# Reordering the end of cross attention in a two-attention and experts kernel

## Chip, cores, metric

The kernel runs on one core of one Trainium2 chip. The metric is the device time of one execution in microseconds. All data is float32; products that need more than one pass are split into a high part and a low part by hand ("hi" and "lo"), and `product` (L41 to L45) issues three matmuls for one: hi by hi, hi by lo, lo by hi.

## The reference, cut to what matters

The reference is one transformer layer over x (8 batches, 128 tokens, 512 features): cross attention to a context of 2048 tokens, then a differential self attention, then a mixture of eight experts, each on a layer norm of x and added to x. The change lies in the end of the first and the start of the second.

```python
q = (LN(x) @ wq.T + bq)       # 8 x 128 x 512, 16 heads of 32
k = ctx @ wk.T + bk           # 8 x 2048 x 512
v = ctx @ wv.T + bv
attn = softmax(q @ k.T / sqrt(32))
x = x + (attn @ v) @ wo.T + bo
lam = exp(sum(lq1 * lk1)) - exp(sum(lq2 * lk2)) + 0.8     # per head
x = x + differential_attention(LN(x), lam, rms_scale, ...)
x = x + experts(LN(x), ...)
```

## The kernel before

Cross attention is one stage (`cross_attention`). Its work is cut into 32 slots: slot m is batch m // 4 and head group m % 4 (four heads). A slot has four chunks of 512 keys, so there are 128 chunks; chunk n belongs to slot n // 4. Each chunk passes through these steps:

- scores on PE (`column_scores`, L852): 32 matmuls into the one PSUM tile `psS`;
- a running maximum on VectorE (L1083, L1086): four instructions;
- the move of the scores to SBUF on ScalarE (L1029), into one of seven buffers; then `psS` is free;
- subtraction of the maximum on VectorE (L1050), exponential on ScalarE (L1012);
- value product on PE (`outputs`, L866), accumulated over the four chunks of a slot in `psO`. The denominators come from sums on GpSimd (L761, L766) and a matmul per slot (L889) up to slot 27, and for the last four slots (`TAIL`) from matmuls of their own (L880), two by two with the value products.

The maximum of a slot is turned on PE (M, L897), reduced on VectorE (L1059), spread on ScalarE (L1007), turned back (B, L897) and copied to `mb` (L980). A slot is finished by a reciprocal (L1071) and a product (L1075) on VectorE, and a copy with the value bias on ScalarE (L1019), whose result is stored to a scratch tensor.

Nothing plans this at run time. Each engine's block runs over the same counter `beat`, and within a beat issues its steps in the order in which they are written. The functions `score_step`, `move_step`, `exp_step`, `value_steps`, `normal_slot` and the like say which chunk or slot has a step in this beat. Each engine works through its own queue in order and waits on semaphores. While projections of new keys and values run, they fill PE. From beat `LATE` (slot 32 of the projections, which isn't there) on, only ten score steps are left (chunks 118 to 127), and the room is used for the output projection: the output weight is turned in four blocks (W, `turn_weight`, L904) at the beats in `W_BEAT`, evicted by ScalarE (L984, L985) and split by GpSimd (L745); the attention output of batches 0 to 6 is loaded back from the scratch tensor, split by ScalarE (L999, beats in `O_BEAT`) and GpSimd (L751), and projected by PE (Y, `project_tile`, beats in `Y_BEAT`) into a work bank, which ScalarE evicts (L989). From `LATE` on two banks are used in turn, as the third holds the denominators. GpSimd adds bo to x (L741) and at the end adds the projected tiles to it (`add_tile`, L514).

The next stage, `output_projection`, begins when all engines have ended the first. It projects the tile of batch 7, makes the statistics and the layer norm in two halves (`Norm`, L166 to L212), turns the result (L1096) and splits it (L1215, L1226). Lambda (`lam_*`) is computed in it too. Then come the projections of the self attention (L1336 and on).

## Time and profile before

| | us |
|---|---|
| median of 3 runs | 1677.9 |
| lowest and highest | 1677.11, 1684.54 |
| the profiled execution | 1679.28 |
| its span | 1677.5 |
| PE busy in the span | 1608.8 (96%) |
| VectorE busy | 1166.9 (70%) |
| ScalarE busy | 954.1 (57%) |
| GpSimd busy | 932.3 (56%) |

PE is nearly full over the span as a whole, but not everywhere: from 1047 to 1176 us, where cross attention ends and the next stage runs, it is busy 90 of 129 us. This is the part that the change touches. In the profile PE is TensorE, DVE is VectorE, ACT is ScalarE and POOL is GpSimd; the granted clock of TensorE is a share of its full speed.

### The profile page before, as it was taken

The numbers are of one execution on the slowest core, as the hardware profiler recorded it, in microseconds if no ns is written. First come the engines' busy times: TensorE is split into PE (matmuls) and PEld (weight loads), VectorE is DVE, ScalarE is ACT, GpSimd is POOL, SyncE is SP. The second block draws the span as 40 slices with busy tenths as digits, with TensorE's granted clock in tenths as the row PEclk, the third lists the DMA queues.
The fourth block names the chain that finished last, engine by engine and source line by source line (L and its number), as shares of the span: only waits on it lengthen the run. The fifth ranks groups of instructions, "written<-read, shape, count | busy, mean of one in ns | idle before, by whom it ended". The sixth has DMA issues, their size and how long they took to land. (4 is left out here: it accounts for less than half of the span.)

```text
span 1677.5 us, 36990 instructions
## 1 busy us (share of the span) xinstructions
PE 1608.8 (96%) x15556; PEld 1302.3 (78%) x15556; DVE 1166.9 (70%) x1506; ACT 954.1 (57%) x1445; POOL 932.3 (56%) x498
## 2 busy tenths in 40 slices
PE   7999999999999999999999999677998899999999
PEld 6788888888888888888888888566886677777787
DVE  6137888888888888888888887756434677653322
ACT  4347677777677776777776776753102777630000
POOL 1227788788888878888887885322000344522220
PEclk9999999999999999999999999778999999899999
DMA  8422222222222222222222211203432111211001
GB/s 179 96 40 39 35 42 36 36 38 40 39 38 38 36 36 41 40 36 38 38 39 37 42 23 61 74 3 108 163 88 88 58 45 52 66 51 50 29 22 51
DMA packets 333876, 88.61 MB, mean 53 GB/s; under 512 B 284656, under 2 KB 317168, under 8 KB 333712
## 3 DMA queue, kind: packets, MB, share of 16 engines
q1 hardware_dynamic: 333712, 86.26, 23.0%
q8 instruction: 123, 2.02, 0.5%
q14 instruction: 41, 0.34, 0.1%
HBM read 71.60 MB, written 14.61 MB: 51 GB/s over the span
## 5 line engine op out<-in xcount | busy, mean ns | idle before, releaser
L766 POOL TENSOR_TENSOR b_acc<-b_acc,b_s 128x1024 f32<-128x1024 f32 x168 | 562.8, 3350 | 12.4 <-ACT b_s L1012 5.5
L1050 DVE TENSOR_TENSOR b_s<-b_s,b_mb 128x2048 f32<-128x2048 f32 x128 | 395.9, 3094 | 32.5 <-ACT b_mb L980 32.5
L1086 DVE TENSOR_TENSOR b_mx<-b_psS,b_mx 128x512 f32<-128x512 f32 x480 | 330.8, 689 | 103.0 <-PE b_psS L852 90.0
L1012 ACT ACTIVATE b_s<-b_s 128x2048 f32<-128x2048 f32 x128 | 244.3, 1909 | 13.8 <-DVE b_s L1050 10.6
L1029 ACT ACTIVATE b_s<-b_psS 128x2048 f32<-128x2048 f32 x128 | 241.1, 1884 | 15.9 <-DVE b_mx L1086 15.9
L43 PE MATMUL b_work<-wvT,cT 128*128 128x512 f32 x496 | 203.2, 410 | 0.0
L43 PE MATMUL b_work<-cT,wkT 128*128 128x512 f32 x496 | 200.2, 404 | 1.7 <-POOL b_ones L732 1.7
L44 PE MATMUL b_work<-cT,wkT 128*128 128x512 f32 x496 | 194.3, 392 | 0.0
L44 PE MATMUL b_work<-wvT,cT 128*128 128x512 f32 x496 | 194.2, 392 | 0.0
L45 PE MATMUL b_work<-wvT,cT 128*128 128x512 f32 x496 | 193.4, 390 | 0.0
L45 PE MATMUL b_work<-cT,wkT 128*128 128x512 f32 x496 | 193.2, 389 | 0.0
L735 POOL TENSOR_TENSOR cT<-cin,cT 128x512 fp32r<-128x512 f32 x120 | 155.8, 1299 | 54.7 <-ACT cT L1004 54.7
L952 ACT ACTIVATE b_kT<-b_work,b_bk 128x512 f32<-128x512 f32 x124 | 85.4, 689 | 141.1 <-PE b_work L45 141.1
L852 PE MATMUL b_psS<-b_q,b_kT 32*128 32x128 f32 x4096 | 152.9, 286 | 12.2 <-ACT b_s L1029 12.1
L852 PEld LDWEIGHTS b_psS<-b_q,b_kT 32*128 32x128 f32 x4096 | 128.4, 189 | 38.1 <-issue 38.1
L761 POOL TENSOR_TENSOR b_acc<-b_s 128x1024 f32<-128x1024 f32 x28 | 68.7, 2452 | 129.5 <-PE b_psO L889 127.6
L866 PE MATMUL b_psO<-b_s,v_sb 128*32 128x128 f32 x4096 | 128.1, 276 | 0.6 <-issue 0.6
L866 PEld LDWEIGHTS b_psO<-b_s,v_sb 128*32 128x32 f32 x4096 | 109.4, 111 | 22.7 <-issue 22.6
L43 PEld LDWEIGHTS b_work<-cT,wkT 128*128 128x128 f32 x496 | 93.0, 187 | 27.5 <-POOL b_ones L732 2.1
L1040 DVE STREAM_TRANSPOSE cin<-cin 128x512 f32<-128x512 f32 x120 | 83.8, 699 | 41.7 <-DMA b_bv<-in_L_xattn_bv 19.3
L43 PEld LDWEIGHTS b_work<-wvT,cT 128*128 128x128 f32 x496 | 93.0, 188 | 24.5
L1846 ACT ACTIVATE e_sm<-e_psS,e_low 128x128 f32<-128x128 f32 x256 | 89.9, 382 | 34.5 <-DVE e_low L1921 34.5
(315 smaller groups left out, 2815.8 us busy)
## 6 DMA issues: line engine op xcount, KB each, us to landing
cin<-in_ctx SPq DMA_DIRECT2D x496, 64.0 KB, 2.4
experts_sb<-in_L_ffn_expert_w SPq DMA_DIRECT2D x8, 1024.0 KB, 5.4
q_scratch<-d_st SPq DMA_DIRECT2D x16, 256.0 KB, 2.3
k_scratch<-d_st SPq DMA_DIRECT2D x16, 256.0 KB, 2.3
e_q<-q_scratch SPq DMA_DIRECT2D x16, 256.0 KB, 2.7
k_sb<-k_scratch SPq DMA_DIRECT2D x16, 256.0 KB, 2.9
b_kT<-in_x SPq DMA_DIRECT2D x4, 512.0 KB, 7.5
q_scratch<-a_q SPq DMA_DIRECT2D x8, 256.0 KB, 2.3
```

The source lines that it names most:

```text
L43: nc.tensor.matmul(out, lhs[0], rhs[0], start=first, stop=False)
L44: nc.tensor.matmul(out, lhs[0], rhs[1], start=False, stop=False)
L45: return nc.tensor.matmul(out, lhs[1], rhs[0], start=False, stop=last)
L735: nc.gpsimd.tensor_tensor(cT[1][:, p % 2, k, :], cin[:, 1, k % 2, :], f32(cT[0][:, p % 2, k, :]), ALU.subtract).then_inc(split_done, 1)
L766: nc.gpsimd.tensor_tensor(acc[:, :, :], acc[:, :, :], s[:, buf, 2 * i:2 * i + 2, :], ALU.add).then_inc(sum_done, 1)
L852: last = nc.tensor.matmul(psS[:, j, t * P:(t + 1) * P], kT[h, at + t * P:at + (t + 1) * P], q[h, m % 3, :], start=True, stop=True)
L866: last = nc.tensor.matmul(psO[j * HD:(j + 1) * HD, 0:P], v[:, at + j * HD:at + (j + 1) * HD], s[:, n % BUFS, i, j * P:(j + 1) * P], start= ...
L1012: nc.scalar.activation(part, part, ACT.Exp, scale=SCALE).then_inc(exp_done, 1)
L1029: nc.scalar.activation(s[:, n % BUFS, :, :].rearrange("p t (j q) -> p t j q", j=HG), psS[:, :, :].rearrange("p j (t q) -> p t j q", t=CHUN ...
L1050: nc.vector.tensor_tensor(s[:, n % BUFS, :, :], s[:, n % BUFS, :, :], mb[:, :].rearrange("p (o n) -> p o n", o=1).broadcast_to([P, CHUNK, ...
L1086: nc.vector.tensor_tensor(mx[:, :, :], part, mx[:, :, :], ALU.max).then_inc(mx_done, 1)
L1846: last = nc.scalar.activation(sm[:, hf, i, j % 2, u, :], psS[:, j, u, :], ACT.Exp, bias=low[:, hf, j, u:u + 1], scale=-1.0, accum_out=sums ...
```

## The change

- On PE, from beat `LATE` on the scores of a beat are issued ahead of its value products and denominators.
- On ScalarE the evictions of W and Y and the high halves of O go behind the move of the scores in a beat, where they stood at its head.
- The beats of W, O and Y are others. W comes four beats earlier.
- Tiles 0 to 5 and not 0 to 6 are projected in cross attention; tiles 6 and 7 in the next stage. Tiles 0 to 3 are evicted by ScalarE and added by GpSimd as before (0 and 1 in the late beats), tiles 4 and 5 are added straight out of PSUM by VectorE.
- The last maximum is reduced ahead of a subtraction, not behind it.
- The last chunk is subtracted and exponentiated in two halves, and its denominators are issued ahead of its value products.
- The lambda loads, product, sum and exponential, and a first use of the square root, are in cross attention; statistics of tiles 0 to 3 too, where it was 0 and 1. `Lambda` holds the tensors.

```diff
-        W_BEAT = {0: LATE + 5, 1: LATE + 5, 2: LATE + 7, 3: LATE + 7}
-        O_BEAT = {0: LATE + 8, 1: LATE + 9, 2: LATE + 12, 3: LATE + 13, 4: LATE + 15, 5: LATE + 17, 6: LATE + 20}
-        Y_BEAT = {0: LATE + 12, 1: LATE + 16, 2: LATE + 19, 3: LATE + 20, 4: LATE + 21, 5: LATE + 23, 6: LATE + 25}
-        TILES = B - 1
+        W_BEAT = {0: LATE + 1, 1: LATE + 1, 2: LATE + 3, 3: LATE + 3}
+        O_BEAT = {0: LATE + 5, 1: LATE + 7, 2: LATE + 9, 3: LATE + 11, 4: LATE + 13, 5: LATE + 17, 6: LATE + 21}
+        Y_BEAT = {0: LATE + 8, 1: LATE + 12, 2: LATE + 16, 3: LATE + 18, 4: LATE + 20, 5: LATE + 23}
+
+        TILES, ADDED = B - 2, 4
+
+        def parts(n):
+
+            if n < SLOTS * CHUNK - 1:
+                return [slice(0, CHUNK)]
+            return [slice(0, CHUNK // 2), slice(CHUNK // 2, CHUNK)]
...
@@ SP, at beat LATE + 2, behind the loads of o_sb
+                    for i, name in enumerate(("lq1", "lq2", "lk1", "lk2")):
+                        sp.dma_start(consts.lam_in_sb[:, i, :], w_next[name]).then_inc(consts.lam_in, 16)
...
@@ GpSimd
-                    for t in {LATE: (0, 1), LATE + 2: (2, 3), LATE + 4: (4, 5), LATE + 6: (6, 7)}.get(beat, ()):
-                        bias(t)
-                    for k in {LATE + 8: (0, 1), LATE + 10: (2, 3)}.get(beat, ()):
-                        weight_lo(k)
-                    for t in {LATE + 12: (0, 1), LATE + 14: (2, 3), LATE + 16: (4,), LATE + 18: (5,)}.get(beat, ()):
-                        output_lo(t)
-                if beat == LATE + 20:
+                    for work_of, n in {
+                            0: ((bias, 0), (bias, 1), (bias, 2)), 2: ((weight_lo, 0), (weight_lo, 1), (bias, 3)),
+                            4: ((weight_lo, 2), (weight_lo, 3)), 6: ((output_lo, 0), (bias, 4), (bias, 5)),
+                            8: ((bias, 6), (bias, 7), (output_lo, 1)), 10: ((output_lo, 2),),
+                            12: ((output_lo, 3), (add, 0)), 14: ((output_lo, 4),),
+                            16: ((add, 1),), 18: ((output_lo, 5),)}[beat - LATE]:
+                        work_of(n)
+                if beat == LATE + 22:
                     output_lo(6)
 
-            pool.wait_ge(sub_done, SLOTS * CHUNK)
-            for t in range(4):
-                add_tile(nc, pool, shared, t)
+            pool.wait_ge(sub_done, SLOTS * CHUNK + 1)
+            for t in range(2, ADDED):
+                add(t)
...
@@ PE
+            def last_outputs(n):
+
+                for i in range(0, CHUNK, 2):
+                    pe.wait_ge(exp_done, n + 1 + i // 2)
+                    for t in range(i, i + 2):
+                        last = tile_denominators(n, t)
+                    if i + 2 == CHUNK:
+                        last.then_inc(last_sums, 1)
+                    for t in range(i, i + 2):
+                        last = tile_outputs(n, t)
+                last.then_inc(pv_done, 1)
...
             for beat in range(FIRST, LAST):
+                if beat >= LATE and (n := score_step(beat)) is not None:
+
+                    column_scores(n)
                 for n in value_steps(beat):
-                    outputs(n)
+                    if n < SLOTS * CHUNK - 1:
+                        outputs(n)
+                    else:
+                        last_outputs(n)
                 if (m := sum_slot(beat)) is not None and m < TAIL:
                     denominators(m)
-                if (n := score_step(beat)) is not None:
+                if beat < LATE and (n := score_step(beat)) is not None:
                     column_scores(n)
...
@@ ScalarE: evictions of W, of Y below ADDED, and the O halves now behind the move in a beat; at the end
+            act.wait_ge(consts.lam_step, 2)
+            nc.scalar.activation(consts.lam_e[:, :], consts.lam_s[:, :], ACT.Exp).then_inc(consts.lam_exp, 1)
+            nc.scalar.activation(norm.root[:, :], ident[:, 0:B], ACT.Sqrt)
...
@@ VectorE
+            def add_tile(t):
+                dve.wait_ge(work_full, RING["Y", t, 0] + 1)
+                dve.wait_ge(shared.bo_done, t + 1)
+                nc.vector.tensor_tensor(x1[:, t, :], work[BANK["Y", t, 0]][:, :], x1[:, t, :], ALU.add).then_inc(y_added, 1)
...
             for beat in range(FIRST, LAST):
+                if (m := spread_slot(beat)) == SLOTS - 1:
+                    reduce_maximum(m)
                 if (n := exp_step(beat)) is not None:
...
-                if (m := spread_slot(beat)) is not None:
+                if (m := spread_slot(beat)) is not None and m < SLOTS - 1:
+                    reduce_maximum(m)
                 if (m := normal_slot(beat)) is not None:
                     if m == SLOTS - 1:
+                        for t in range(ADDED, TILES):
+                            add_tile(t)
+                        dve.wait_ge(consts.lam_in, 16 * 4)
+                        nc.vector.tensor_tensor(consts.lam_p[:, :, :], consts.lam_in_sb[:, 0:2, :],
+                                                consts.lam_in_sb[:, 2:4, :], ALU.mult).then_inc(consts.lam_step, 1)
                         for t in range(2):
...
+                    elif m < SLOTS - 1:
+                        dve.wait_ge(pv_done, (m + 1) * CHUNK)
                     else:
-                        dve.wait_ge(pv_done, (m + 1) * CHUNK)
+                        dve.wait_ge(last_sums, 1)
...
@@ the next stage, PE
+            for g in range(G):
+                last = product(nc, bank[0][:, :], [a[:, g, :] for a in shared.o_half[THERE % 4 - 2]],
+                               [a[:, g, :] for a in woT], g == 0, g == G - 1)
+            last.then_inc(full, 1)
             pe.wait_ge(o_lo, 2)
...
@@ the next stage, VectorE
-            for t in range(2, THERE):
-                dve.wait_ge(shared.y_done, t + 1)
-                norm.tile_stats(x1, t)
-            dve.wait_ge(lam_in, 16 * 6)
...
-            for t in range(THERE, LAST):
-                dve.wait_ge(shared.y_done, t + 1)
+            for t in range(B // 2, THERE):
                 norm.tile_stats(x1, t)
-            dve.wait_ge(shared.bo_done, B)
-            dve.wait_ge(full, 1)
-            nc.vector.tensor_tensor(x1[:, LAST, :], bank[0][:, :], x1[:, LAST, :], ALU.add).then_inc(lo_done, 1)
-            dve.wait_ge(lo_done, 1)
-            norm.tile_stats(x1, LAST)
+            for t in range(THERE, B):
+                dve.wait_ge(full, t - THERE + 1)
+                nc.vector.tensor_tensor(x1[:, t, :], bank[t - THERE][:, :], x1[:, t, :], ALU.add).then_inc(lo_done, 1)
+                dve.wait_ge(lo_done, t - THERE + 1)
+                norm.tile_stats(x1, t)
```

## Rows read from the trace of the kernel before

**Rows 1.** Busy time of each engine by stage; columns: busy us (instructions), clock, DMA share, GB/s.

```profile
1047.57:1116.37 68.80, 49.41 (x989) 42.30 (x985) 49.26 (x53) 45.21 (x43) 21.39 (x17) 0.78 0.18 47
1116.37:1129.67 13.30, 8.40 (x64) 6.74 (x61) 5.57 (x7) 6.96 (x7) 2.55 (x2) 0.87 0.00 0
1129.67:1151.84 22.17, 20.39 (x425) 17.64 (x424) 12.78 (x10) 10.28 (x10) 5.02 (x4) 1.00 0.06 15
1151.84:1169.33 17.49, 7.88 (x28) 6.41 (x28) 13.56 (x43) 4.79 (x11) 4.62 (x7) 0.79 0.68 240
1169.33:1176.08 6.75, 4.19 (x19) 3.81 (x19) 5.86 (x14) 2.39 (x4) 0.00 (x0) 0.50 0.01 2
```

**Rows 2.** Waits by total, 1047 to 1178 us: total us, times, longest.

```profile
ACT b_s L1029 <- DVE b_mx L1086: 15.9, 7, 3.0
...
PE b_psS L852 <- ACT b_s L1029: 12.1, 6, 5.0
```

**Rows 3.** Timeline of PE: start us, us, engine, line, operation, count, idle before.

```profile
1053.82 1.17 PE L852 MATMUL b_psS<-b_q,b_kT 32*128 32x128 f32 x32 [1.03 <-ACT b_s L1029]
...
1059.98 2.09 PE L852 MATMUL b_psS<-b_q,b_kT 32*128 32x128 f32 x32 [0.82 <-ACT b_s L1029]
...
1070.25 1.09 PE L904 MATMUL b_work<-ident,wo_sb 128*128 128x128 f32 x8
...
1076.75 1.93 PE L866 MATMUL b_psO<-b_s,v_sb 128*32 128x128 f32 x32 [0.27 <-issue]
...
1091.94 0.77 PE L43 MATMUL b_work<-woT,b_o_half 128*128 128x512 f32 x1 [0.49 <-POOL b_o_half L751]
...
1097.20 1.08 PE L866 MATMUL b_psO<-b_s,v_sb 128*32 128x128 f32 x32
...
1140.05 0.39 PE L43 MATMUL b_work<-woT,o_half 128*128 128x512 f32 x1
...
1142.86 1.08 PE L866 MATMUL b_psO<-b_s,v_sb 128*32 128x128 f32 x32
```

**Rows 4.** Timeline of VectorE, cross attention's end.

```profile
1036.41 3.21 DVE L1050 TENSOR_TENSOR b_s<-b_s,b_mb 128x2048 f32<-128x2048 f32 x1 [1.12 <-ACT b_mb L980]
...
1047.70 0.96 DVE L1071 RECIPROCAL b_rD<-b_psO 128x128 f32<-128x128 f32 x1 [1.21 <-PE b_psO L889]
...
1055.05 2.87 DVE L1086 TENSOR_TENSOR b_mx<-b_psS,b_mx 128x512 f32<-128x512 f32 x4 [1.09 <-PE b_psS L852]
1057.84 2.28 DVE L1050 TENSOR_TENSOR b_s<-b_s,b_mb 128x2048 f32<-128x2048 f32 x1
1060.04 0.68 DVE L1059 TENSOR_REDUCE b_top<-b_work 128x4 f32<-128x512 f32 x1
```

**Rows 5.** Timeline of GpSimd, its last additions of the steady part.

```profile
1035.06 6.79 POOL L766 TENSOR_TENSOR b_acc<-b_acc,b_s 128x1024 f32<-128x1024 f32 x2 [5.30 <-ACT b_s L1012]
```

**Rows 6.** Timeline of ScalarE in the ring.

```profile
1057.95 1.88 ACT L1029 ACTIVATE b_s<-b_psS 128x2048 f32<-128x2048 f32 x1 [2.05 <-DVE b_mx L1086]
...
1061.29 1.90 ACT L1012 ACTIVATE b_s<-b_s 128x2048 f32<-128x2048 f32 x1
1063.15 0.60 ACT L980 ACTIVATE b_mb<-b_work 128x512 f32<-128x512 f32 x1
...
1067.28 0.60 ACT L985 ACTIVATE woT<-b_work 128x512 fp32r<-128x512 f32 x1
```

**Rows 7.** Timelines of VectorE and ScalarE in the next stage.

```profile
1153.81 1.35 DVE L1232 TENSOR_TENSOR c_oT<-b_o,c_oT 128x128 fp32r<-128x128 f32 x1
1155.08 1.27 DVE L166 BATCH_NORM_STATS2 c_norm_stats<-x 128x6 f32<-128x512 f32 x2
1157.14 0.21 DVE L1238 TENSOR_TENSOR c_lam_p<-c_lam_in 16x64 f32<-16x64 f32 x1 [0.79 <-DMA e_rs<-in_L_attn_rms_scale]
...
1164.01 0.67 DVE L1252 TENSOR_TENSOR x<-c_ps,x 128x512 f32<-128x512 f32 x1
...
1157.85 1.28 ACT L208 ACT_TABLE_LOAD   x1
```

More of the change, by code:

```diff
@@ L749, in output_lo @@
                 pool.wait_ge(shared.o_hi, t + 1)
+                if t == 1:
+                    pool.wait_ge(shared.bo_done, B)
                 hi, lo = o_half[t % 4]
@@ L811, in wait_evicted @@
                         pe.wait_ge(shared.wo_hi, m + 1)
+                    elif kind == "Y" and m < ADDED:
+                        pe.wait_ge(shared.y_moved, m + 1)
                     elif kind == "Y":
-                        pe.wait_ge(shared.y_moved, m + 1)
+                        pe.wait_ge(y_added, m - ADDED + 1)
                     else:
@@ L863, in outputs @@
                 for i in range(CHUNK):
[L864 to L869 removed]
+                    last = tile_outputs(n, i)
@@ new lines, in tile_outputs @@
+            def tile_outputs(n, i):
+                m, c = divmod(n, CHUNK)
+                b, g = divmod(m, G)
+                at = value_places(b, c * CHUNK + i)[g]
+                for j in range(HG):
+                    last = nc.tensor.matmul(psO[j * HD:(j + 1) * HD, 0:P],
+                                            v[:, at + j * HD:at + (j + 1) * HD],
+                                            s[:, n % BUFS, i, j * P:(j + 1) * P],
+                                            start=c == 0 and i == 0, stop=c == CHUNK - 1 and i == CHUNK - 1)
+                return last
@@ L883, in chunk_denominators, with tile_denominators @@
+            def tile_denominators(n, i):
+                c = n % CHUNK
+                for j in range(HG):
+                    last = nc.tensor.matmul(work[BANKS - 1][j * HD:(j + 1) * HD, 0:P], ones[:, :],
+                                            s[:, n % BUFS, i, j * P:(j + 1) * P],
+                                            start=c == 0 and i == 0, stop=c == CHUNK - 1 and i == CHUNK - 1)
                 return last
```

161 lines of the change are left out of this document (80 added, 81 removed).

## Prediction

> I write S118 to S127 for the last ten score steps (32 score matmuls each, L852), O for one chunk's value product with its denominators, Y for the projection of one batch tile, W for the turning of one block of the output weight, M29 and B29 for the turns of the maxima of slot 29. A step's "move" is ScalarE's copy of the scores out of PSUM (L1029).
>
> **What bounds the kernel now.** I read first the busy time by stage. The change touches only the end of cross attention and the stage behind it, and five stretches hold it [rows 1]: S118 to S127 (68.80 us, granted clock 0.78), S127 to the subtraction of chunk 124 (13.30), from there to the last copy of the attention output (22.17), the next stage to its first low half (17.49), and its rest (6.75). No engine is full in the first: PE 49 us of 69, VectorE 49, ScalarE 45. So it is bound by a chain, and the waits name it: ScalarE waits for the maxima, PE for the move [rows 2]. There is one PSUM tile for scores, so the chain is a ring: scores, maxima, move, next scores. The shortest turn stands in the timeline: S119 starts at 1053.82, the maxima at 1055.05 and last 2.87, the move runs from 1057.95 for 1.88, S120 starts at 1059.98 [rows 3, 4, 6]. That is 1.23 + 2.90 + 2.03 = 6.16 us; nine turns are 55.4 of the 68.8. The other 13.4 us are turns in which the next scores stood behind something else on PE, or the move behind something on ScalarE. The dearest is Y0 with two O in front of S125: Y0 alone is 5.26 us, from 1091.94 to 1097.20, at the low clock [rows 3].
>
> The clock matters here. Scores take 1.17 us (1053.82) or 2.09 us (1059.98, after PE had waited), twelve Y matmuls 2.81 us (1140.05 to 1142.86) or 5.26; the first half of an O takes 1.08 or 1.93 us [rows 3]. These are the 2.4 and the 1.2 GHz level.
>
> **The ring after the change.** I follow it turn by turn at full clock.
> - *Start.* S118 is issued ahead of the denominators of slot 27 and begins earlier by their 0.6 us, at 1046.99. But VectorE has the reciprocal of slot 27 in front of the maxima of 118, and that now waits for denominators behind the scores. Before, it started at 1047.70 and lasted 0.96 [rows 4]; now it starts near 1048.8, when both are done, and with the 0.3 us product behind it the maxima start at 1050.05, where they had started at 1048.90. The turn lasts 8.0 instead of 6.16: 1.8 lost.
> - *S120.* The turns W2 and W3 now stand ahead of S120, and W3 needs the PSUM bank of M29, which is free only when VectorE has subtracted chunk 115 (2.28) and reduced the maximum (0.68) [rows 4]. Eight matmuls of this kind took 1.09 [rows 3], so W3 costs 0.55. From the end of the maxima this is 2.28 + 0.68 + 0.55 = 3.5 against the move's 2.03: 1.4 lost. Queued behind PE's new wait is S120, and all engines wait for S120.
> - *The same place, a shared resource.* VectorE's subtraction takes 2.28 us alone but 3.21 at 1036.41, where GpSimd ran its additions [rows 4, 5]. The low halves of the weight now run on GpSimd just behind S119, beside the subtraction of 115. The rows bound it by 0 and 0.93; the additions cover nearly the whole subtraction, so I take the upper end, 1.0 rounded. Elsewhere the subtraction has about 1 us of room in a turn, and I cost it at nothing. (The Trainium skill, "GPSIMD: programming the Q7 cores", section Limitations, says GpSimd shares an SBUF port with VectorE. It speaks against moving additions to run beside VectorE work; the two rows agree with it.)
> - *S121.* ScalarE has exp of 115 (1.90 [rows 6]), four evictions of W2 and W3 (0.60 each, less some overlap) and the copy of mb (0.60) ahead of move 120: together 4.4 from the spread copy's end, against scores and maxima of 4.1. 0.3 lost.
> - *S122 to S127.* The O behind S121, S123 and S125 (two of them are four halves at 1.08, the first matmuls of one over the last of another: 3.5 us at full clock [rows 3]) end before the move does: scores 1.1 + 3.5 = 4.6 of 6.16. A Y behind scores ends at 1.1 + 2.8 = 3.9. O and Y halves and their evictions now lie behind the move on ScalarE. So what stood in front of S121, S123, S125 and S127 before is covered by the maxima and the move. The second O of each pair is needed seven chunks later only. Reciprocals at 122 and 126 cost 0.1 each: 0.2. GpSimd's queue has the low half for Y0 behind the weight's and S121, done near 1071 where Y0 wants it at 1076: nothing.
>
> Sum: 55.4 + 1.8 + 1.4 + 1.0 + 0.3 + 0.2 = 60.1.
>
> *The clock in the ring.* Before, three of the ten scores took the long time, S120 [rows 3] and two others like it. After, PE does the same work in fewer microseconds, with waits of 1.5 to 3 us in nearly each turn. A low S costs 0.92. I take four of nine: 3.5. The bounds are 0 and the slow rival below (8.3 and pushes). So the ring takes 63.6 and S127 starts at 1046.99 + 63.6 = 1110.6, against 1116.37: **5.8 gained**.
>
> **From S127 to the subtraction of chunk 124.** Before, M31 was issued right behind the maxima. Now two O and Y3 are ahead of it: 1.15 + 3.5 + 2.8 + 0.5 = 7.95 us after S127, where the maxima are there at 4.1. So 3.3 us are lost at M31. In return Y2 (about 4.3 of the stretch) and the evictions are gone from the front, and the maximum is reduced ahead of the subtraction. On: 0.7 reduction, 2.25 subtraction of 123, 1.95 exp (it stands ahead of mb on ScalarE), 0.55 mb: 13.4. Before 13.30 [rows 1]. **Nothing gained**; 2.3 lost if Y3 runs at the low clock.
>
> **To the last output copy.** Before 22.17. PE has two Y fewer in it ahead of the O, ScalarE no Y evictions that hold up exp. VectorE sets the end: subtractions 124 and 125 (4.5), reciprocal and product (1.25), subtraction 126 and the two halves of 127 (2.28 + 2.35, the split costs about 0.1) are 10.4. The two adds of tiles 4 and 5 (0.67 each, as the add at 1164.01), four statistics (1.27 for two [rows 7]), and two small steps make 4.2: VectorE reaches the last reciprocal at 14.6. PE is done at 13.45 (last exp half at 11.9, then three quarters of a chunk), so the early denominators hide nothing: the reciprocal would wait for VectorE's own queue. 0.96 + 0.3 + 0.4 behind: 16.3. **5.9 gained.** What is late next is VectorE, by 1.2 us.
>
> **A new piece before the stage's end.** ScalarE now does the lambda exponential, a table load and a root behind its last copy, and all engines meet at the end of the stage: 0.2 + 1.28 [rows 7] + 0.2. **1.7 lost.** Bounds 1.5 and 1.7 by the rows. (The Trainium skill, "ScalarE: Activation LUTs", section What ACT_TABLE_LOAD costs, puts a drain of 1.38 us beside the load, in all about 2.66. By it the loss would be 3.1 and the sum 1.4 us worse. The load at 1157.85 starts right behind an exponential and shows no such time.)
>
> **The next stage.** VectorE is its chain. Out of it go: two statistics 1.27, the lambda product with its wait for a transfer (0.79 + 0.5), the 1.28 of the table load, and 0.9 of the low halves, which ran beside GpSimd's additions (128 columns took 1.35) [rows 7]. In come: one more add (0.67 + 0.1), and a wait for tile 7, as PE has 24 matmuls where it had 12. They start 0.4 us into the stage at the low clock: the first twelve end at 5.6, the others at 8.4 to 9.5, where VectorE wants them at 8.2: 0.2 to 1.3; and a memset moved into the chain, 0.15. 4.7 - 0.8 - 0.15 = 3.8, less that wait, is 3.6 to 2.5; it hangs on when PE's clock comes up, and I take the middle: **3.1 gained**. The lambda loads, four issues on SP's queue, go behind the loads of the attention output and ahead of the store of slot 28, for which that queue would have waited anyway: nothing. The weight loads for the stage behind it start as before at its beginning, and nothing in rows says they'd be late. The last stretch of 6.75 stays.
>
> **The sum.** 5.8 + 0 + 5.9 - 1.7 + 3.1 = 13.1 us. The profiled execution took 1679.28 with a span of 1677.5, the median of the runs is 1677.9, 1.4 below it. 1679.3 - 13.1 = 1666.2, less 1.4: **1665 us** in terms of the median. Within 0.5% means within 8.4 us, about what a measurement of this kernel can tell from no change.
>
> **Rivals.**
> - *Clock free.* PE's work lies in shorter gaps, so that every S runs at full clock. For it: nearly every turn now has matmuls in it, and S119, with products in front of it, was fast. Against it: gaps of 1.5 to 3 us stay in each turn, and S120 was slow [rows 3]. 3.5 better: 1661.5. Chance 0.17.
> - *Clock and neighbours dearer.* About a third of the PE work of the rival below is slow, or a product pair at the low clock pushes the next S (scores 2.0 + two O 6.6 = 8.6 against a turn of 7.1: 1.5 each, five of them), and GpSimd slows more subtractions. 5 to 10 worse: 1670 to 1675. Chance 0.18.
> - *Slower than before: PE at the low clock all through.* Scores before products leave PE waiting in every turn, so it never comes up. Then nine S cost 8.3 instead of 3.5, pushes 6.0 in the ring, and behind S127 PE itself becomes the bound: scores 2.05, four pairs of O at 6.6, Y3 to Y5 at 5.26, M31, B31 and the wait between them 3.4, are 47.6 us to the last product against my 26.9 (13.4 + 13.45), of which VectorE's tail hides 1.2: 19.5 more. 4.8 + 6.0 + 19.5 = 30.3: 1695. The kernel is slower once about 13 of these 30 come. Against it: the granted clock was 0.78 in the ring with its long waits and 1.00 in the stretch with the fewest [rows 1], and at the low clock a pair of O fills its turn and leaves no gap. Chance 0.05.
> - *Forecast*, 1661 to 1669: 0.60.
>
> **Chances.** Faster by over 0.5% (below 1669.5): 0.60 + 0.17 = 0.77. Within: 0.18. Slower: 0.05. The range 1659 to 1674 takes in the first two cases with 2 us for what I haven't seen, and most of the third.
>
> **What would show it.** S118 to S127 in 60 to 66 us, turns without a low clock at 6.2, and S119 and S120 late by 1.8 and 2.4. M31 about 8 us after S127. The reciprocal of slot 31 not waiting for PE. A table load before the stage's end and 1.7 us between the last output copy and the next stage. The next stage at 14.4 up to the first low half. The prediction is wrong if PE's waits before S don't end by the move, if the clock is well under 0.8 in the ring, or if the steady loop ahead of it, untouched here, has another length.

## The result and the profile after

| | before | changed |
|---|---|---|
| median of 7 runs, us | 1683.73 | 1670.15 |
| lowest and highest | 1677.11, 1685.1 | 1666.02, 1672.92 |
| profiled execution | 1679.28 | 1670.15 |
| its span | 1677.5 | 1668.4 |

The ratio is 0.9931, with a 95% interval of 0.9908 to 0.9954: 0.69% faster, or 11.6 us of 1678 to 1684. Run again beside the experiments below, the changed kernel came to 0.9952 (0.9934 to 0.9970). Both kernels have two levels some 5 us apart, which experiment 10 looks into. One execution of the kernel before, taken beside experiments 1 and 2, was a slow one of 2024.4 us at a granted clock of 0.743 and is in no ratio.

The busy time by stage, as in [rows 1], cut at the same events (S118, S127, subtraction of 124, end of the last output copy, first low half, first matmul of the self projections). Columns: busy us (instructions) of PE, PEld, DVE, ACT, POOL, then clock, DMA share, GB/s:

```profile
1047.56:1111.78 64.22, 45.66 (x885) 38.86 (x885) 51.96 (x53) 44.90 (x42) 26.08 (x19) 0.87 0.18 50
1111.78:1126.97 15.19, 13.65 (x216) 11.57 (x220) 5.80 (x7) 8.27 (x9) 1.30 (x1) 0.89 0.01 2
1126.97:1144.04 17.07, 13.77 (x384) 11.93 (x372) 16.43 (x17) 8.76 (x9) 5.48 (x3) 1.00 0.06 17
1144.04:1158.98 14.94, 9.08 (x40) 7.38 (x40) 11.21 (x39) 4.79 (x12) 0.60 (x4) 0.89 0.68 238
1158.98:1165.52 6.54, 3.76 (x18) 3.55 (x19) 5.81 (x14) 2.39 (x4) 0.00 (x0) 0.74 0.27 101
```

Against [rows 1]: 68.80 became 64.22, 13.30 became 15.19, 22.17 became 17.07, 17.49 became 14.94, 6.75 became 6.54. From S118 to the self projections 128.51 us became 117.96: 10.55 less. S118 comes at the same time in both (1047.57 and 1047.56), although it no longer waits for 0.58 us of denominators: the steady part took 0.57 longer in this execution (in the second profile of the changed kernel, experiment 10, S118 starts at 1046.94). The span is 9.1 shorter, so 1.46 us of the 10.55 were lost behind the changed stages.

The ring on PE, with the start and length of the scores and what they waited for ([rows 3] has the like of before):

```profile
1047.56 1.17 PE L867 MATMUL b_psS<-b_q,b_kT 32*128 32x128 f32 x32
1048.66 0.65 PE L922 MATMUL b_psO<-b_acc,b_ones 128*32 128x128 f32 x16
...
1055.49 2.09 PE L867 MATMUL b_psS<-b_q,b_kT 32*128 32x128 f32 x32 [5.16 <-ACT b_s L1050]
...
1064.16 0.65 PE L937 MATMUL b_work<-ident,wo_sb 128*128 128x128 f32 x4 [0.35 <-DVE b_top L1086]
1064.75 1.17 PE L867 MATMUL b_psS<-b_q,b_kT 32*128 32x128 f32 x32
...
1070.92 2.09 PE L867 MATMUL b_psS<-b_q,b_kT 32*128 32x128 f32 x32 [2.67 <-ACT b_s L1050]
...
1085.08 2.09 PE L867 MATMUL b_psS<-b_q,b_kT 32*128 32x128 f32 x32 [2.94 <-ACT b_s L1050]
1087.09 1.94 PE L904 MATMUL b_psO<-b_s,v_sb 128*32 128x128 f32 x32
1088.80 1.93 PE L913 MATMUL b_work<-b_s,b_ones 128*32 128x128 f32 x32
...
1092.71 0.66 PE L930 MATMUL b_work<-ident,b_mx 128*128 128x128 f32 x4
1093.29 1.17 PE L867 MATMUL b_psS<-b_q,b_kT 32*128 32x128 f32 x32
...
1111.78 2.09 PE L867 MATMUL b_psS<-b_q,b_kT 32*128 32x128 f32 x32 [2.02 <-ACT b_s L1050]
```

The scores now wait for the move (ACT b_s L1050) in most turns, as they should. The nine turns are 7.93, 9.26, 6.17, 7.08, 7.08, 8.21, 6.17, 6.16, 6.16 us. The first two are the two places that were forecast: the denominators behind S118, and W3, which waits for the reduced maximum, ahead of S120. Four of the ten scores take 2.09 us, three of them in the nine turns (S119, S121, S123) and the fourth, S127, behind them. The turn of 8.21 is the pair of products at the low clock that holds up S124. It also holds the move of chunk 123 up, which needs the buffer of seven chunks before and so waits for one of these products:

```profile
1090.86 1.88 ACT L1050 ACTIVATE b_s<-b_psS 128x2048 f32<-128x2048 f32 x1 [3.13 <-PE b_work L913]
```

VectorE in the ring and behind it, with GpSimd where the two meet:

```profile
1060.43 2.93 DVE L1112 TENSOR_TENSOR b_s<-b_s,b_mb 128x2048 f32<-128x2048 f32 x1
...
1074.38 2.53 POOL L750 TENSOR_TENSOR x<-x,b_bo 128x512 f32<-128x512 f32 x2
1075.85 3.20 DVE L1112 TENSOR_TENSOR b_s<-b_s,b_mb 128x2048 f32<-128x2048 f32 x1
...
1080.16 2.86 DVE L1159 TENSOR_TENSOR b_mx<-b_psS,b_mx 128x512 f32<-128x512 f32 x4
...
1121.55 0.69 DVE L1086 TENSOR_REDUCE b_top<-b_work 128x4 f32<-128x512 f32 x1 [4.75 <-PE b_work L930]
...
1126.97 5.59 DVE L1112 TENSOR_TENSOR b_s<-b_s,b_mb 128x2048 f32<-128x2048 f32 x2 [2.54 <-ACT b_mb L1019]
1127.47 2.95 POOL L763 TENSOR_TENSOR o_half<-o_sb,o_half 128x512 fp32r<-128x512 f32 x1 [12.20 <-ACT o_half L1072]
```

VectorE waits 4.75 us for the turned maximum, which PE has behind two O and Y3. The subtractions 124 and 125 take 5.59 us where before two took 4.49, 2.28 being the time of one alone [rows 4]:

```profile
1129.67 4.49 DVE L1050 TENSOR_TENSOR b_s<-b_s,b_mb 128x2048 f32<-128x2048 f32 x2 [6.39 <-ACT b_mb L980]
```

The subtraction of 115 took 2.93 instead of 2.28. Both lie beside work of GpSimd. At the end the first subtraction keeps its pace (the second begins 2.2 us behind it, at 1129.18), GpSimd's instruction beside it takes 2.95 us where others of its kind take 1.28, and the second subtraction, begun before GpSimd ended at 1130.42, takes 3.38.

There is a third such place, in the turn S122 to S123, which took 7.08 us although S122 ran at full clock. The subtraction beside GpSimd's two additions took 3.20 us, the reciprocal and the product of slot 28 stand behind it, and so the maxima of 122 start at 1080.16, where S122, begun at 1078.00, would have allowed 1079.23 (1.23 behind, as in [rows 3, 4]). These 0.92 us are what the subtraction was too long. The second profile has the same (3.19 us, a turn of 7.07).

ScalarE at the end of the stage, with the piece that the change adds:

```profile
1143.64 0.40 ACT L1040 ACTIVATE b_o<-b_oq,b_bv 128x128 f32<-128x128 f32 x1 [3.84 <-DVE b_oq L1148]
1143.95 0.19 ACT L1076 ACTIVATE c_lam_e<-c_lam_s 16x2 f32<-16x2 f32 x1
1144.15 1.28 ACT L1077 ACT_TABLE_LOAD   x1
1145.45 0.21 ACT L1077 ACTIVATE c_norm_root<-ident 128x8 f32<-128x8 f32 x1
1146.13 0.53 ACT L1293 ACTIVATE c_oT<-o_sb 128x384 fp32r<-128x384 f32 x1 [0.47 <-ACTq L512]
```

From the end of the last output copy (1144.04) to the next stage's first instruction are 2.09 us; before, the copy ended at 1151.84 and the next stage's first instruction of ScalarE came at 1152.42, 0.58 later. So the piece costs 1.5.

### The profile page after: what moved, and what is told of

Read it like the earlier page. It is cut to its first block and busy times, and to the rows that moved or that the text cites. A ratio compares the mean times of both kernels' runs of the same rounds, so it can differ in the third digit from the quotient of the medians.

```text
span 1668.4 us, 36971 instructions
## 1 busy us (share of the span) xinstructions
PE 1603.7 (96%) x15541; PEld 1298.4 (78%) x15556; DVE 1171.9 (70%) x1510; ACT 954.5 (57%) x1444; POOL 932.4 (56%) x495
## 5 line engine op out<-in xcount | busy, mean ns | idle before, releaser
L1112 DVE TENSOR_TENSOR b_s<-b_s,b_mb 128x2048 f32<-128x2048 f32 x129 | 400.3, 3105 | 28.9 <-ACT b_mb L1019 28.9
L1050 ACT ACTIVATE b_s<-b_psS 128x2048 f32<-128x2048 f32 x128 | 241.3, 1885 | 16.5 <-DVE b_mx L1159 11.8
```

The costliest lines, as they stand in the source:

```text
L1050: nc.scalar.activation(s[:, n % BUFS, :, :].rearrange("p t (j q) -> p t j q", j=HG), psS[:, :, :].rearrange("p j (t q) -> p t j q", t=CHUN ...
L1112: nc.vector.tensor_tensor(s[:, n % BUFS, tiles, :], s[:, n % BUFS, tiles, :], mb[:, :].rearrange("p (o n) -> p o n", o=1) .broadcast_to([P ...
```

## Experiments

All stretches are cut as above: "ring" is S118 to S127, "middle" S127 to the subtraction of 124, "end" from there to the end of the last output copy, "next" to the first low half. In the changed kernel they are 64.2, 15.2, 17.1 and 14.9 us; "the piece" is all of it, from S118 to the self projections. Experiments 3 to 9 are one execution each. A time of a whole execution can't settle a microsecond here, so the stretches of one profile are the measure.

**1. PE's old order alone (e1).** The scores of a late beat go behind the products again, all else stays as changed:

```diff
-                if beat >= LATE and (n := score_step(beat)) is not None:
+                if beat >= LAST and (n := score_step(beat)) is not None:
                     column_scores(n)
...
-                if beat < LATE and (n := score_step(beat)) is not None:
+                if (n := score_step(beat)) is not None:
                     column_scores(n)
```

> The changed kernel with PE's old order (value products and denominators ahead of the scores of a beat), all else as changed. Changed kernel: S118 to S127 64.2 us, S127 to the subtraction of 124 15.2, from there to the last output copy 17.1. Theory (the order on PE is worth time because Y and two O together don't fit under the maxima and the move): S121 0.9, S123 1.3, S125 2.3, S127 1.3 us later, so the ring 68 to 70; M31 comes after Y3 alone, so the next stretch is about 12; in all 1 to 3 us slower than the changed kernel. Rival (the order costs clock, the gain is from ScalarE's order and the new beats alone): ring at 64 or shorter, with more scores at 1.17 us. Second rival (the whole gain is PE's order): back to 1678 or more.

Ratio to the kernel before 0.9945 (0.9917 to 0.9972). Its busy time by stage, ring and middle:

```profile
1048.22:1121.30 73.08, 54.01 (x1001) 45.71 (x997) 52.08 (x53) 47.36 (x44) 26.07 (x19) 0.79 0.17 44
1121.30:1131.64 10.34, 7.92 (x68) 6.14 (x64) 5.66 (x6) 5.38 (x6) 1.31 (x1) 1.00 0.01 2
```

The ring is 8.9 us longer (clock 0.79 and not higher: the rival that the order costs clock falls; so does the second, back to 1678, with a median of 1672.2), the middle 4.9 shorter, and S118 to the self projections takes 121.64, 3.7 more than in the changed kernel. The direction and the mechanism were as expected, both stretches by more than I had put, and the sum just above 1 to 3.

**2. ScalarE's old order alone (e2).** The block that evicts W and Y and makes the O halves stands at the head of a beat again:

```diff
+                for k in late_units(W_BEAT, beat - 1):
...
+                for t in [t for t in late_units(Y_BEAT, beat - 1) if t < ADDED]:
...
+                for t in late_units(O_BEAT, beat):
...
                 if (x0 := transposed(beat)) is not None:
...
                                          ACT.Copy).then_inc(s_moved, 1)
-                for k in late_units(W_BEAT, beat - 1):
...
```

> The changed kernel with ScalarE's old order (evictions of W and Y and the O halves at the head of a beat, ahead of exp and move). Theory: a move then waits for a Y that ends late: move 124 by 1.8 us (Y1), move 126 by 1.0 (Y2), small ones elsewhere; ring 66.5 to 68, the stretches behind it within 1 us. Rival (PE's order alone makes the gain, ScalarE has room): ring 64 to 65.

Ratio 0.9948 (0.9933 to 0.9964). Ring 68.76, middle 15.36; S118 to the self projections 122.62, 4.7 more. Its timeline of ScalarE shows a move (L1070 here) behind an eviction that waits for a Y:

```profile
1097.64 0.60 ACT L1028 ACTIVATE o_sb<-b_work 128x512 f32<-128x512 f32 x1 [1.29 <-PE b_work L45]
...
1098.65 1.87 ACT L1070 ACTIVATE b_s<-b_psS 128x2048 f32<-128x2048 f32 x1
```

The rival (ScalarE has room) falls; the ring is 0.8 above the upper end that I gave.

**3. Both old orders (e12).** The edits of 1 and 2 together: what is left of the change are mainly the new beats, the two tiles in the next stage, the halves and lambda.

> PE's and ScalarE's orders both as before the change, the rest (beats, tiles, halves) as changed. With PE's order alone put back the ring was 73.1 us, with ScalarE's alone 68.8, in the kernel before 68.8. Theory (a Y in front of the scores on PE also holds the move up on ScalarE, so the two orders remove the same delays in part): 73 to 76. Rival (they add): 77 to 79. Rival (each hurts only with the other one new): 69.

Its busy time by stage, ring, middle and end:

```profile
1048.08:1118.86 70.78, 50.40 (x1000) 43.14 (x997) 52.90 (x53) 45.85 (x44) 23.96 (x19) 0.81 0.17 46
1118.86:1129.20 10.34, 7.90 (x64) 6.17 (x61) 5.66 (x7) 6.54 (x7) 1.31 (x1) 0.91 0.01 2
1129.20:1146.07 16.87, 15.52 (x401) 13.52 (x399) 16.37 (x17) 8.75 (x9) 5.48 (x3) 0.95 0.07 18
```

None of the three guesses holds: the ring is 70.8, below 73 and above 69. Over the whole piece it takes 119.45 us, against 117.96 and 116.77 in two profiles of the changed kernel and 128.51 before. So the two orders that the list of the change puts first are by this one execution together worth 1.5 to 2.7 us (the two profiles of the changed kernel are themselves 1.2 apart), and the rest of it 9.1. Each order alone, with the other new, costs more (3.7 and 4.7) than both (1.5). The rows show why ScalarE's old order costs little once PE's is old too:

```profile
1115.34 0.60 ACT L1028 ACTIVATE o_sb<-b_work 128x512 f32<-128x512 f32 x1 [3.90 <-PE b_work L45]
...
1116.35 1.87 ACT L1070 ACTIVATE b_s<-b_psS 128x2048 f32<-128x2048 f32 x1
...
1118.86 1.17 PE L867 MATMUL b_psS<-b_q,b_kT 32*128 32x128 f32 x32
```

The move stands behind an eviction that waits for a Y, and still ends at 1118.22, while PE has products ahead of the next scores until 1118.86; at the two other Y of the ring the move ends 0.6 us ahead of them as well. Only the turn S119 to S120 is longer for another reason than the clock (8.85 against 8.00 in experiment 1). That the ring is even 2.3 shorter than in experiment 1 lies in the clock of PE's products: the two O behind S120, for one, take 3.7 us here and 5.3 there. And what the orders take out of the ring (70.8 to 64.2) comes back in the middle (10.3 to 15.2) for the most part; there PE has the products and tiles that it no longer does in the ring. Against the kernel before, this kernel has a ring 2.0 us longer, a middle 3.0 shorter, an end 5.3 shorter and a next stage, with its rest, 2.8 shorter.

**4. The start of the ring (e3).** The denominators of slot 27 go ahead of S118 again:

```diff
-                if beat >= LATE and (n := score_step(beat)) is not None:
+                if beat > LATE and (n := score_step(beat)) is not None:
...
-                if beat < LATE and (n := score_step(beat)) is not None:
+                if beat <= LATE and (n := score_step(beat)) is not None:
```

> Scores ahead of products only behind the first late beat: the denominators of slot 27 go ahead of S118 again. Changed kernel: S118 at 1047.56, S119 7.9 us later. Theory (the reciprocal of slot 27 in front of the maxima makes the first turn long): S118 0.6 later, first turn 6.2 to 6.9, S119 1.1 us earlier against the end of the last value projection; the rest of the ring unchanged, so S127 0.8 to 1.7 earlier. Rival (the first turn is long from the low clock of S119 alone): first turn 7.1 or more.

The first turn is 6.24 and not 7.93, as expected by the theory, at a S118 that waits 0.58 for the denominators: 1.1 net. S119 took 1.58 us, between the two levels, and the ring 61.55. The ring is 2.7 us shorter than in the first profile of the changed kernel and 1.4 shorter than in the second, where 0.8 to 1.7 were expected. The first turn accounts for 1.7; the turn behind it was 9.55 long, and the rest comes from the turns of S122 and S123 (6.36 and 6.99 instead of 7.08 and 8.21).

**5. The weight behind S120 (e5).**

```diff
-        W_BEAT = {0: LATE + 1, 1: LATE + 1, 2: LATE + 3, 3: LATE + 3}
+        W_BEAT = {0: LATE + 1, 1: LATE + 1, 2: LATE + 5, 3: LATE + 5}
```

> W2 and W3 at beat LATE + 5, behind S120. Changed kernel: S119 to S120 9.3 us. Theory (S120 waits for W3, which waits for the bank of M29, behind a subtraction that GpSimd slows): that turn 7.1 with S119 at the low clock; ring 62 to 63 instead of 64.2. Rival (ScalarE's four evictions then fall into a later turn and delay it as much): ring 64 and a longer turn S121 to S122. If S120 drops to the low clock, 0.9 of it is given back.

The turn S119 to S120 is 7.54 instead of 9.26, and no later turn grew: 6.16, 6.85 and then five of 6.16, with no slow score behind S119.

```profile
1047.59:1106.86 59.27, 42.67 (x886) 36.27 (x885) 51.26 (x53) 44.78 (x42) 32.05 (x19) 0.91 0.20 54
```

The row is the ring's busy time. It is 4.95 shorter than in the first profile of the changed kernel (3.7 than in the second), and shorter than the 62 to 63 of the theory. 1.7 are the wait for W3. Of the rest 2.05 are the turn of S123, at full clock here (0.9 against the second profile), and 0.9 the turn of S122, in which VectorE is not late this time, as the subtraction ahead of its reciprocal took 2.69 us and not 3.20. The rival (evictions delay a later turn) falls.

**6. The last maximum ahead of Y3 (e4).**

```diff
-        Y_BEAT = {0: LATE + 8, 1: LATE + 12, 2: LATE + 16, 3: LATE + 18, 4: LATE + 20, 5: LATE + 23}
+        Y_BEAT = {0: LATE + 8, 1: LATE + 12, 2: LATE + 16, 3: LATE + 19, 4: LATE + 20, 5: LATE + 23}
```

> Y3 one beat later, so that M31 stands ahead of it on PE. Theory (the turn of the last maximum behind Y3 is on the path): M31 3.0 to 3.5 us earlier behind S127, the stretch from S127 to the subtraction of 124 11.7 to 12.5 instead of 15.2, the next one 17 to 18. Rival (PE's work is the bound from S127 on, so order doesn't matter): the first shrinks and the second grows by the same.

M31 comes 6.40 us behind S127 instead of 9.13, the middle is 13.01 instead of 15.19, the end 17.57 instead of 17.07. A gain of 2.2, of which 0.5 goes: between theory and rival, nearer to the theory (against the second profile 2.3 and 0.7). It fell short because the products ahead of M31 ran mostly at the low clock in this execution: from 1111.53 to 1116.82, 5.3 us where 3.6 are enough.

**7. The root left in the next stage (e6).** The last line of ScalarE's cross attention goes:

```diff
-            nc.scalar.activation(norm.root[:, :], ident[:, 0:B], ACT.Sqrt)
```

> The first root and its table load leave the end of cross attention; the load then falls ahead of the root in the next stage. Theory: 1.5 us less between the last output copy and ScalarE's next instruction (0.6 instead of 2.1), 1.3 more in VectorE's chain of the next stage: last output copy to first low half 14.9 becomes 14.7, a draw. Rival (the next stage waits for PE's tile 7, not for VectorE, so the load is hidden there): 13.4 to 13.8. Rival by the load's drain: 1.4 us more saved than that.

"Next" is 13.44 us, not 14.94: the rival's number, though not by its reason. The table load stands in the next stage, but costs next to nothing there. The timeline of ScalarE:

```profile
1142.75 0.53 ACT L1292 ACTIVATE c_oT<-o_sb 128x384 fp32r<-128x384 f32 x1 [0.29 <-PEq L512]
...
1143.49 1.28 ACT L208 ACT_TABLE_LOAD   x1
1144.79 0.20 ACT L208 ACTIVATE c_norm_root<-c_norm_veps 128x4 f32<-128x4 f32 x1
```

and on VectorE

```profile
1145.03 0.18 DVE L187 RECIPROCAL c_norm_rstd<-c_norm_root 128x4 f32<-128x4 f32 x1 [0.46 <-ACT c_norm_root L208]
```

It starts as soon as ScalarE is free and runs while VectorE makes the low halves and the aggregates; VectorE waits 0.46 us for the root where it waits 0.27 with the table there. Before the change the load was exposed:

```profile
1159.39 0.18 DVE L187 RECIPROCAL c_norm_rstd<-c_norm_root 128x4 f32<-128x4 f32 x1 [1.21 <-ACT c_norm_root L208]
```

ScalarE had lambda's exponential in front of it, which had waited 4.49 us for VectorE. Moving that one ahead was enough; the early root costs 1.5 and saves 0.2. The load is 1.28 us in each of these places, and in each the next instruction of ScalarE starts 0.02 us behind it.

**8. GpSimd beside VectorE (e8).** The low half of tile 6 goes behind GpSimd's last adds:

```diff
-                if beat == LATE + 22:
-                    output_lo(6)
...
                 add(t)
+            output_lo(6)
```

> GpSimd makes the low half of tile 6 behind its last adds and not beside the subtraction of 124. Theory (the two engines slow each other): subtractions 124 and 125 together 4.5 us instead of 5.6, the stretch to the last output copy 16.0 instead of 17.1. Rival (PE is as late as VectorE at the end, and gaps in its own issue set it): 17 unchanged.

The subtractions 124 and 125 take 4.49 us again and the end 15.73 instead of 17.07 (16.83 in the changed kernel's second profile): the theory's numbers. In eight other profiles with the old place of this low half the end is 16.83 or 16.84 (experiments 1, 2, 4, 5, 7 and 10, and both of 9), so the 1.1 us are the 1.1 of the two subtractions. This execution also had S127 and all that is behind it at full clock: M31 at 7.60 and the middle 13.66. "Next" was 15.61: VectorE waited 0.58 us for PE's tile 7, as twelve of the stage's matmuls ran at the low clock where it was eight in the first profile.

**9. The clock (e7, e10).** Matmuls of the identity, written to columns of the output bank that nobody reads, fill PE's waits ahead of S119, S123 and S127. First 30, 16 and 10, then 16, 9 and 5:

```diff
             for beat in range(FIRST, LAST):
+                if (fill := {LATE + 2: (16, 28), LATE + 10: (9, 29), LATE + 18: (5, 30)}.get(beat)) is not None:
+                    pe.wait_ge(od_free, fill[1])
+                    for _ in range(fill[0]):
+                        nc.tensor.matmul(psO[:, 2 * P:3 * P], ident[:, :], ident[:, :], start=True, stop=True)
                 if beat >= LATE and (n := score_step(beat)) is not None:
```

> Extra matmuls of the identity into unused columns of the output bank (30 ahead of S119, 16 ahead of S123, 10 ahead of S127), read by nobody, to fill PE's waits. Theory (the clock falls because PE waits): S119, S123 and S127 take 1.17 and not 2.09 us; ring 64.2 less 2.8 is 61.4, the stretch behind it 0.7 shorter as the products run at full clock too. Rival (the clock doesn't matter on the path, or falls for another reason): ring 64 or more, scores still 2.09.

The thirty took 6.96 us where I had reckoned 4.2 (0.14 each, from the turns), and held S119 up by 2.1; the ring was 66.23. The number says nothing on the clock's price, though S119, S123 and S127 took 1.17, as expected. S120 and S121 took 2.09 here: PE waited 2.05 us for the reduced maximum ahead of W3, and W3 already ran at the low clock.

> As the run with filling matmuls, with about half of them (16, 9 and 5), as one took 0.23 and not 0.14 us and they held S119 up by 2.0 us. Theory: S119, S123 and S127 at 1.17 us without being held up; S119 at 7.9 us behind S118; ring 61 to 62, the stretch from S127 to the subtraction of 124 13.7 and not 15.2. Rival: ring 64 or more.

The timeline of PE with the smaller number:

```profile
1050.80 3.84 PE L953 MATMUL b_psO<-ident 128*128 128x128 f32 x32 [0.38 <-DVE b_oq L1152]
1055.57 1.17 PE L867 MATMUL b_psS<-b_q,b_kT 32*128 32x128 f32 x32 [0.94 <-ACT b_s L1054]
```

and its busy time by stage, ring and middle:

```profile
1047.64:1108.51 60.87, 49.12 (x946) 42.79 (x945) 52.31 (x53) 44.96 (x42) 26.09 (x19) 0.94 0.19 53
1108.51:1122.17 13.66, 12.12 (x216) 10.27 (x220) 5.79 (x7) 8.27 (x9) 1.32 (x1) 1.00 0.01 2
```

With work in PE's wait S119 starts where it did (7.93 behind S118) and takes 1.17; only S121, ahead of which nothing was filled in, is slow. Ring 60.87, middle 13.66: 3.4 and 1.5 less than in the changed kernel's profile, with 2.1 and 1.7 less than in its second. So a slow S119 does come from PE's wait: it took 2.09 us in all seven profiles with a wait of 5.2 us ahead of it, 1.58 and 1.33 in the two with 4.05, and 1.17 in the two with that wait filled. What the clock costs in these two stretches, 3.8 to 4.9 us, rests on one execution, and part of it can be chance: without any filling experiment 8 has the middle of 13.66, and experiment 5 a ring that with its 1.7 us for W3 added back is 61.0.

**10. The changed kernel again (e11), and the gain that seemed lost.**

> The changed kernel as it is, beside the others on this chip. Theory (about 1.5 us of the gain seemed lost behind the changed stages, in the attention stage, by chance of the clock and not by the change): S118 to the self projections 114 to 118.5, and what comes behind it between 500.5 and 508 in both kernels, without regard to the change. Rival (the change makes the later stages slower): more than 502 again each time.

Ring 62.95, middle 15.34, end 16.83; from S118 to the self projections 116.77. What comes behind took 507.9 us in this profile and 502.9 in the first, from the same program; before 501.4; in the other experiments from 500.5 (e1, e5, e7) to 507.9 (e2). In windows of 20 us and more the granted clock of the two agrees within 0.01 in all but one, the third 20 us of the self attention's stage, here first in the first and then in the second profile of the changed kernel:

```profile
1315.52:1335.52 20.00, 16.70 (x156) 13.41 (x157) 15.64 (x43) 16.31 (x77) 9.83 (x17) 1.00 0.17 54
```

```profile
1313.71:1333.71 20.00, 17.08 (x136) 14.04 (x134) 11.81 (x31) 13.31 (x59) 9.01 (x16) 0.74 0.09 27
```

At a granted clock of 0.74 PE gets through 136 matmuls there, at 1.00 through 156. Experiment 2, with 507.9 behind the stages, has 0.74 in that place too; experiment 5, with 500.5, and the profile before have 1.00. Variants of the changed kernel took 500.5 us behind the stages, less than the 501.4 before, so the 1.46 us behind the changed stages are chance and no work of the change. It is also a source of the changed kernel's two levels; for the kernel before, whose upper level has no profile, that is likely and not shown.

**11. Five edits together (e9).** Those of 4, 5, 6, 7 and 8.

> The changed kernel with five edits at once: denominators of slot 27 ahead of S118, W2 and W3 behind S120, M31 ahead of Y3, the low half of tile 6 behind the last adds, no root and table load at the end of cross attention. If their sizes add up (S118 to the stage of the self projections 118.0 us in the changed kernel; 1.7 for the start, 2.2 and fewer slow scores for the weight, 2.2 for M31, 1.1 for the subtraction, 1.5 for the root): 106.5 to 109, the execution 9 to 11 us below the changed kernel, ratio to the kernel before 0.986 to 0.989. If the edits share a cause (the gains of the weight and the start were luck of the clock): 110 to 112, ratio 0.990.

Its five stretches, in the order of the changed kernel's:

```profile
1048.34:1106.19 57.85, 41.70 (x872) 35.33 (x869) 52.12 (x53) 44.21 (x42) 32.08 (x19) 0.94 0.20 56
1106.19:1119.13 12.94, 10.74 (x182) 9.30 (x183) 5.80 (x7) 8.16 (x9) 1.29 (x1) 0.87 0.01 1
1119.13:1136.69 17.56, 16.21 (x407) 14.22 (x405) 15.36 (x17) 8.86 (x9) 3.78 (x3) 1.00 0.07 19
1136.69:1150.12 13.43, 8.00 (x40) 6.21 (x40) 11.22 (x40) 4.57 (x11) 0.60 (x4) 0.91 0.76 267
1150.12:1156.87 6.75, 3.97 (x19) 3.60 (x19) 5.85 (x14) 2.39 (x4) 0.00 (x0) 0.68 0.25 91
```

Ratio 0.9908 (0.9886 to 0.9931), where the changed kernel in the same comparison has 0.9952: it beats both kernels. The medians are 1663.56 and 1672.52. The piece takes 108.53 us, inside 106.5 to 109. Two of the five don't add: with M31 ahead of Y3 the end is 17.56 and not 15.7, as PE then has Y3 and Y4 in front of the products of slot 30. VectorE waits 1.70 us for that slot's denominators, 0.59 in experiment 6, so the 1.1 us of the faster subtraction only lengthen this wait; and PE is busy 16.2 of these 17.6 us. The ratio came out above the 0.989 expected, and the gain over the changed kernel, 8.96 us by the medians, just under the 9 to 11. The profiled execution is one of the short ones (1661.66 us, 503.03 behind the stages); the longest of the six took 1670.16, and as it has no profile, why is open.

## Why the prediction was right

Forecast were 13.1 us off (1665 us), in a range of 1659 to 1674; the ratio is worth 11.6 (7.7 to 15.4 by its interval), and the median of the runs was 1670.15. The 1665 was reckoned from a median of 1677.9, at the lower level of the kernel before, and the seven runs of the comparison have it at 1683.73, at the upper. Lowest against lowest the gain is 11.1 us, highest against highest 12.2. I had not reckoned with levels, and on which one a median falls is luck. Step by step, the first profile first and the second behind it:

| step | forecast, us | measured, us |
|---|---|---|
| ring, S118 to S127 | 63.6 | 64.22, 62.95 |
| first turn | 8.0 | 7.93, 7.94 |
| S119 to S120 | 6.16 + 1.4 + 1.0 = 8.6, at the low clock 9.5 | 9.26, 9.25 (low) |
| slow scores in the ring | 4 of 9 | 3, 3 (and S127 in the first) |
| S122 to S123 | 6.16 + 0.1 | 7.08, 7.07 |
| M31 behind S127 | 7.95 | 9.13, 9.28 |
| middle | 13.4 | 15.19, 15.34 |
| end | 16.3 | 17.07, 16.83 |
| early root | 1.7 | 1.5 |
| next, with it | 1.7 + 14.4 | 14.94, 15.47 |
| rest | 6.75 | 6.54, 6.18 |

- **The ring** was right in its sum, and experiments 4 and 5 show both causes that were named for the long first turns. The 1.0 for GpSimd beside the subtraction of 115 was 0.65 (2.93 against 2.28). Elsewhere errors cancel. Three slow scores and not four cost 2.8 and not 3.5; the 0.3 for ScalarE's queue at S121 does not show. Against that, I had given every later subtraction about 1 us of room and cost GpSimd there at nothing. In the turn of S122 the reciprocal stands behind the subtraction and the room is gone: 0.92 us. A push by a slow pair of products, which the dearer rival had as 1.5 us each, came once, at S124, as 1.1 (8.21 against 7.08 for a turn with a slow score). That the sum fits to 0.7 us is in part luck.
- **The middle** is the mis-sized term: 1.8 to 1.9 us too short. I had named 2.3 us for a low clock there and taken none of it. With PE at full clock all through (e7, e8, e10) the middle is 13.66 or 13.67 and M31 7.6 behind S127, against 13.4 and 7.95. So 1.5 to 1.7 us of the miss are the clock. M31 itself was forecast 0.35 too late at full clock, and the steps behind it 0.6 too short (6.06 us against 5.45).
- **The end**: 0.5 to 0.8 too short. The step that I left out is the low half of tile 6 on GpSimd, which the new beats put beside the subtraction of 124: 1.1 us by experiment 8. I had cost GpSimd beside a subtraction at one place only. Without it the end is 15.73, so the rest of my sum was 0.6 too long. Before the change PE and not VectorE was late here:

```profile
1150.13 0.96 DVE L1071 RECIPROCAL b_rD<-b_work 128x128 f32<-128x128 f32 x1 [3.79 <-PE b_work L880]
```

That two Y fewer take this wait away fits, but was not tried by itself. That the last reciprocal waits for VectorE's own queue held in the second profile. In the first it started at 1142.32, 0.14 us after that queue was free and 0.03 behind the last denominators, which had lost 1.2 us in two gaps of PE; this is the 0.24 between the two ends.
- **The early root** cost what was forecast. What I had not seen is that it is needless: I booked 1.28 us saved in the next stage for the table, and experiment 7 shows that the load would have been hidden there. The gain belongs to moving lambda out of ScalarE's way. The longer switch that the Trainium skill gives ("ScalarE: Activation LUTs", What ACT_TABLE_LOAD costs) did not show: in the trace the root starts 0.02 us behind the load, and the sum without the longer switch was the right one.
- **The next stage** is 1.2 us shorter than forecast in the first profile and 0.6 in the second: PE came up to full clock after eight of its 24 matmuls, and VectorE didn't wait for tile 7 in the one and waited 0.5 in the other.
- **Lost on the way**: 0.57 us in the steady part and 1.46 behind, by chance of the execution (experiment 10). I had named another length of the steady loop as a sign of being wrong; S118 at 1046.94 in the second profile, against the 1046.99 forecast, says that it was none.

The errors in size run against each other: -0.6 (or +0.7) in the ring, -1.8 in the middle, -0.8 at the end, +0.2 and +1.0 in the next stage, +0.2 in its rest. The forecast was 13.1 with S118's earlier start in it; like for like, the stages give 11.1 (128.51 + 0.58 - 117.96) and 12.3.

**Where the explanation stands back.** I had put 5.8 us to the ring and nothing to the middle, as if the orders on PE and ScalarE made the ring's gain for free. The stretches came out nearly so (4.6 and 5.9 us in the ring in the two profiles, -1.9 and -2.0 in the middle), but experiment 3 shows that this is no account of causes: without the two orders the piece is only 1.5 to 2.7 us longer. The larger share, 9.1 us, comes from what is left: less work ahead of the last steps (a tile less for PE, two evictions and adds less for ScalarE and GpSimd), from the beats, and from lambda out of the next stage. How these 9.1 us split among themselves was not tried.

The slower rival (PE at the low clock all through) did not come: the granted clock was 0.87 in the ring (0.89 in the second profile), against 0.78 before. I had feared that scores ahead of products would lower it; with PE's old order it is 0.79 and 0.81 (experiments 1 and 3), so the new order raised it. It is not that PE waits much less: it is idle for 18.6 us of the ring and was for 19.4. What in the new order keeps the clock up was not tried.

## What to carry to other kernels

Where a ring through one buffer bounds a stretch, write down for each turn what stands between its steps on every in-order queue, and price a moved instruction by the wait it carries along: the turn of the weight was 0.6 us of work and 1.7 of delay. Reordering around such a ring moves work behind it, so ask at once what the stretch behind it then waits for. A table load needs no early call if its engine is idle before the first use; it is enough that nothing which waits stands in front of it.

## What the runs showed that I had not expected

- GpSimd's elementwise work cost three times what I had booked, always by one slowed subtraction of VectorE on the path: 0.65 us at the start of the ring, 0.92 at S122, 1.1 at the end, together 2.7 us against 1.0. Only the last was tried by moving it; the other two are read from the rows.
- A few idle microseconds of PE decide more than their length: in one execution, filling 3.8 us of a 5.2 us wait and parts of two smaller ones with useless matmuls went with stretches 3.8 to 4.9 us shorter. A matmul of 128 x 128 in f32 took 0.23 us, a turn of the same size 0.14.
- Whole executions of the same program differ by 5 us, and the one place behind the changed code where their clocks differ is a 20 us stretch, 150 us on, at 0.74 or at 1.00. An experiment's total therefore says little at this size, while its stretches repeat within 0.3 us where the clock is the same (M31 to the subtraction of 124 is 6.05 or 6.06 us in all nine profiles with its order).
- PE has short gaps within groups of small matmuls that wait for nothing the profile shows, 0.3 to 1.2 us each (0.54 and 0.63 in the last products of the changed kernel). What makes them was not tried.
